# Waits that a cache used to drop, and the unfold steps at one per tile

## The reference

```
xn   = layernorm(x)                      # without weights
q1,q2,k1,k2 = xn @ W1_q.T, ...           # 16 heads of 4 numbers each
L_q  = normalize(q1 ^ q2); L_k = ...     # exterior product: 6 numbers a head
P    = softmax(causal(L_q . J6 L_k / sqrt(6)))
attn = (P @ (xn @ W_v.T + b_v)) @ W_out.T + b_out
W_real, W_imag = unfold(G1_R, G2_R), unfold(G1_I, G2_I)   # two 512 x 512 matrices from small cores
ffn  = complex product of xn's halves with W_real, W_imag, + biases
y    = x + attn + ffn
```

## Time and profile before

| what | value |
|---|---|
| three runs, us | 4673.68, 4672.62, 4688.39; median 4673.68 |
| profiled execution, us | 4680.85 |
| span of its slowest core, us | 4679.7 |
| spans of its cores, us | 4645.7 to 4679.7 |
| PE, PEld busy | 60%, 21% |
| DVE, ACT, POOL busy | 30%, 31%, 3% |
| mean granted PE clock | 0.66 |

### The profile page before, as it was taken

How to read it: one execution, slowest core, us unless ns; L and a number is a source line. 1 busy time by engine, 2 the same in 40 slices (tenths; PEclk the granted TensorE clock), 3 DMA queues, 4 the chain that set the end, 5 groups by cost and what they waited for, 6 DMA issues and landing times.

```text
span 4679.7 us, 33896 instructions; the slowest of 8 cores (4645.7 to 4679.7 us)
## 1 busy us (share of the span) xinstructions
PE 2820.8 (60%) x10528; PEld 970.6 (21%) x10528; DVE 1386.5 (30%) x2833; ACT 1474.0 (31%) x1729; POOL 141.3 (3%) x210
## 2 busy tenths in 40 slices
PE   2358555566656755556655855556665686666665
PEld 1114111121112411111211511112211241111112
DVE  5534333322223234332222323432222231111111
ACT  0000144434331034443332014444333204455550
POOL 2200000000000000000000000000000000000001
PEclk9868655567656955567765875556665695555558
DMA  5602201012100311111100040011110031000004
GB/s 112 47 0 67 91 27 34 28 59 68 45 9 7 57 38 32 34 40 67 63 21 11 15 71 28 28 34 59 63 50 7 5 51 32 14 12 14 12 12 74
DMA packets 87133, 180.13 MB, mean 38 GB/s; under 512 B 41760, under 2 KB 42920, under 8 KB 86960
## 3 DMA queue, kind: packets, MB, share of 16 engines
q0 software_dynamic: 56672, 75.38, 8.7%
q1 hardware_dynamic: 30288, 102.58, 7.3%
HBM read 114.36 MB, written 69.73 MB: 39 GB/s over the span
## 4 chain that ended last, share of the span: by engine, by line
PE 44%; DMA 21%; DVE 14%; ACT 12%; issue 7%; DVEq 0%; SPq 0%; ACTq 0%; POOL 0%; POOLq 0%
PE O L609 18%; DMA cdiv<-rscr 10%; DMA y<-ost 7%; PE S L569 7%; PE F L410 5%; ACT exps L592 5%; PE F L446 4%; DMA rscr<-cdiv 3%; DVE oT L651 3%; ACT cdiv L635 3%; ACT cdiv L633 3%; PE F L453 2%; PE F L336 2%; DVE exps L600 1%; PE F L316 1%
## 5 line engine op out<-in xcount | busy, mean ns | idle before, releaser
L592 ACT ACTIVATE exps<-S 128x1024 bf16<-128x1024 f32 (+3 forms) x1280 | 1119.4, 893 | 2046.7 <-PE O L609 1310.1
L609 PE MATMUL O<-exps,vaug 128*65 128x512 bf16 (+3 forms) x2560 | 1030.9, 503 | 807.6 <-DVE oT L651 479.5
L569 PE MATMUL S<-fqp,fkp 6*128 6x512 bf16 (+3 forms) x2560 | 613.2, 488 | 437.8 <-ACT exps L592 431.8
L609 PEld LDWEIGHTS O<-exps,vaug 128*65 128x65 bf16 x2560 | 229.7, 135 | 1244.6 <-issue 1226.0
L651 DVE TENSOR_TENSOR oT<-O,cdiv 64x512 bf16<-64x512 f32 x256 | 175.0, 684 | 895.4 <-DMA cdiv<-rscr 891.3
L569 PEld LDWEIGHTS S<-fqp,fkp 6*128 6x128 bf16 x2560 | 131.9, 97 | 1154.3 <-issue 1151.8
L600 DVE TENSOR_TENSOR exps<-exps,tri 128x256 bf16<-128x256 bf16 x512 | 143.7, 292 | 725.8 <-ACT exps L592 722.8
L515 PE MATMUL S<-wout,oT 128*128 128x512 bf16 x1024 | 252.8, 407 | 100.0 <-DVE ost L524 90.8
L410 PE MATMUL F<-wv,xnT 128*128 128x256 bf16 x2048 | 233.2, 279 | 0.4 <-DVE vaug L422 0.4
L316 PE MATMUL F<-idt,xnst 128*128 128x128 f32 x512 | 119.9, 413 | 146.2 <-DVE xnst L303 146.2
L410 PEld LDWEIGHTS F<-wv,xnT 128*128 128x128 bf16 x2048 | 190.6, 100 | 48.0 <-issue 7.1
(11 more groups left out here) (75 smaller groups left out, 1961.4 us busy)
## 6 DMA issues: line engine op xcount, KB each, us to landing
y<-ost POOLq DMA_DIRECT2D x128, 512.0 KB, 5.3
x2st<-x SPq DMA_DIRECT2D x64, 512.0 KB, 4.3
cdiv<-rscr SPq DMA_DIRECT2D x128, 256.0 KB, 3.6
xst<-x SPq DMA_DIRECT2D x56, 512.0 KB, 4.4
exps<-x SPq DMA_DIRECT2D x8, 512.0 KB, 4.9
wv<-wvT POOLq DMA_DIRECT2D x8, 256.0 KB, 22.9
wout<-woutT POOLq DMA_DIRECT2D x8, 256.0 KB, 23.7
tascr<-qk POOLq DMA_DIRECT2D x16, 128.0 KB, 2.1
```

What stands on the lines that cost most here:

```text
L569: tS.inc(TE.matmul(S_ps[:, ss * 1024 + j * 512 + soff: ss * 1024 + j * 512 + 512], fk_pad[32 * m4:32 * m4 + 6, kt * 128:kt * 128 + 128], f ...
L592: sS.inc(SE.activation(e_out, e_in, AF.Exp))
L609: ins = TE.matmul(O4[:, j * 512 + off:(j + 1) * 512], vaug[:, kt * 1040 + h * 65: kt * 1040 + h * 65 + 65], exp_sb[:, ss * 1024 + j * 512 ...
```

## The change

Two things are changed.

1. `Sem.wait` no longer remembers anything: every call issues its wait. The waits that come back are all fulfilled when the engine reaches them. Counted over the whole program (each core has the same one), there are 2118 more wait instructions:

| engine | waits before | after | where the new ones stand (with the lines of before) |
|---|---|---|---|
| PE | 2582 | 3780 | V_group 260, scores of a pair 256, A2_tile 227, C_scatter 130, FFN_pass1 106, B2_chunk 76, burst_outproj 70, ahead of L609 for O4 32, B1_chunk 25, unf_step 16 |
| DVE | 2375 | 3069 | FFN_pass1 317, A1_tile 182 (127 of them right ahead of L303), emit_divide 128 (ahead of L651), burst_outproj 67 |
| SP | 625 | 772 | emit_divide 143 (127 of them ahead of L640), A1_tile 4 |
| ACT | 1781 | 1860 | emit_divide 48 (ahead of L633) and one more, exp 30 |
| POOL | 276 | 276 | none |

2. The loop over the 16 tiles of batch 0 issues one unfold step behind each tile where it issued two, and `unf_fin` comes after the loop. Before, the 16 steps stood behind tiles 0 to 7 in pairs (F6, then F7), and `unf_fin` behind tile 8. Now tile 0 has a step in F6, tile 1 one in F7, and so on to tile 15.

No arithmetic is added or taken away, and apart from the unfold steps no instruction changes its place.

```
     def wait(self, eng, n=None):
-        v = self.n if n is None else n
-        k = id(eng)
-        if self.lastw.get(k, -1) >= v:
-            return
-        self.lastw[k] = v
-        eng.wait_ge(self.h, v)
+        eng.wait_ge(self.h, self.n if n is None else n)
```

```
         for tt in range(NT):
             A1_tile(0, tt, tt % 2)
             A2_tile(0, tt)
-            for _ in range(2):
-                if unf_steps:
-                    unf_steps.popleft()()
+            if unf_steps:
+                unf_steps.popleft()()
+        while unf_steps:
+            unf_steps.popleft()()
         for ch in range(4):
             B1_chunk(0, ch)
```

More of the change, by code:

```diff
@@ L80, in __init__ @@
         self.n = 0
-        self.lastw = {}
     def inc(self, instr, k=1):
```

## The result

| | before | after |
|---|---|---|
| median of the runs, us | 4678.82 (8 runs) | 4747.44 (8 runs) |
| ratio, 95% interval | | 1.0142 [1.0125, 1.0159] |
| profiled execution, us | 4680.85 | 4746.13 |
| mean of the 8 cores' spans, us | 4662.3 | 4714.3 |

The changed kernel is 1.4% slower; 1.2% was forecast, 4728 us, with 4697 to 4768 as the range. In the profiled executions the slowest core is 65 us later, the mean core 52 us. In some executions, whatever the kernel, the cores of a die are granted a lower clock and take some per cent longer; the ratios leave these out, while the medians of the experiments hold them, so the two can differ by a few us.

A forecast was written before the change was run, and what follows sets the result against it. Handovers, not a busy engine, bound the kernel, with nearly all 128 divisions in the chain. Waits 47 us plus unfold steps 6.9 gave 54 us on the median of 4673.68: 4728 us, range 4697 to 4768.

The forecast's parts named there:

- nearly free: Rival, whole kernel: queues run ahead, so fulfilled waits cost almost nothing and only unfold steps count; 4679 us, chance 0.13.
- divisions: Division of each head pair, 128 in the chain: new waits on SP, DVE and ACT add 20 us.
- PE's waits exposed in attention: Rival, attention: if PE's queue does not run ahead, each of 668 waits costs 0.10 us; 4806 us, chance 0.10.
- opening, waits and unfold steps: Batch 0's 16 tiles: waits add 3.8 us, unpaired unfold steps net 6.9 us.
- q/k stage of batch 0: Serial q/k steps with PE empty before each: new PE waits behind the blocking one add 2.0 us.
- value stages: All four batches: a fulfilled sem_s wait per group of 8 matmuls, 49 groups a batch at full clock, adds 10 us.
- q/k of later batches and PE's other waits in attention: Attention stages: 6 us for later batches' q/k steps, 5 us for PE's scores, C_scatter, A2_tile, O4 and burst waits.
- DVE outside division and opening: DVE's remaining new waits, such as FFN_pass1's: taken as hidden, 0 us.
- FFN and output stages: FFN and output stages of the batches: no change in length, 0 us.
- The zero for FFN_pass1: FFN_pass1: DVE's and PE's new waits fall into time already spent waiting; 0 us, at worst 4.5.
- The gathers: Started at about 210 us instead of 123.22, they hide behind the q/k stage, which moves no data.

The follow-up runs named there:

- the two SP variants: Kernel before with four more fulfilled SP waits at each write of the reciprocal, behind or ahead of the blocking wait: ratio 1.0062 behind, 0.9999 ahead.
- division cached: Changed kernel with the cache back inside emit_divide alone, 320 waits fewer: 4719.9 us, ratio 1.0085.
- values only: Kernel before with the cache off for PE's two waits in V_group alone, 260 extra waits: 4695.84 us, ratio 1.0019.
- PE's waits only: Kernel before with the cache off for PE alone, 1198 of the 2118 waits: 4708.54 us, ratio 1.005.
- DVE's, no division: Kernel before with the cache off for DVE except in the division, 566 extra waits: 4700.76 us, ratio 1.002.
- the waits only: Kernel before with the cache taken out, all 2118 waits, unfold steps left in pairs: 4753.85 us, ratio 1.0161.

## Why the prediction was right

**The price.** The prices had been read from two tiles that differed by one wait and, for SP, from a division: 0.07 us on DVE, 0.10 on PE, 0.06 on SP. They hold, but for SP's, which is 0.05. In tile 1 of the changed kernel two more on DVE made 0.13, one more on PE 0.15 and in tile 2 0.10, and four on SP made 0.20. The trace also keeps the wait instructions themselves, which no view prints. Ahead of L297 in tile 1 they start at 42.08, 42.15, 42.21 and 42.28, 0.07 apart. Ahead of the write at 581.03 SP's start at 580.88, 580.92 and 580.97, 0.05 apart. In core 0's value stage PE's two start at 1521.49 and 1521.60, 0.11 apart.

**The rule of exposure.** The prediction had a new wait cost something only behind the one that blocks. This is shown by three pairs: the changed kernel and its twin with the blocking wait last (4747 and 4665 us with the same number of waits), the two SP variants, and the value stage (347 and 366 matmuls in 40 us). Of the rivals, "nearly free" fails since the divisions add about 0.14 us each and the whole is 66 us. "PE's waits exposed in attention" fails in full (67 us).

**The terms**, in us, in the means over the cores:

| term | worked out | shown by | measured |
|---|---|---|---|
| divisions | 20 | division cached | 20 to 21 |
| opening, waits and unfold steps | 10.7 | stage A | 10.0 |
| q/k stage of batch 0 | 2.0 | stage q/k | 3.9 |
| value stages | 10 | values stages, values only | 15 |
| q/k of later batches and PE's other waits in attention | 6 + 5 | PE's waits only | 14; 9 to 10 by all executions |
| DVE outside division and opening | 0 | DVE's, no division | 10, within the scatter; about 6 by all executions |
| FFN and output stages | 0 | their stages | -14.5 |

The sum of 54 against 52 for the mean core is nearer than its terms, and that is luck: errors of opposite sign met. Values, q/k stage and DVE's waits were put too low by 5, 2 and some 6 us, and that the FFN and output stages get shorter by 14.5 was not foreseen. The measured terms come from different executions and need not add up to 52; with the two taken over all executions they come to about 50. The value term failed in its count of groups at the full clock, taken from one core and one batch; with 64 groups it would have been 13. The q/k term is larger by 2 us than 20 waits of 0.10 explain; why is not settled, though nearly all of it goes away when the blocking wait is last (+0.2), and the stage scatters by up to 1.4. The zero for FFN_pass1, and for L297 in the paced pieces, rested on DVE having slack there, and perhaps it has not.

The metric is the slowest core, and there the change costs 66 us, 12 more than forecast: the prediction added up one chain and had nothing for a spread between the cores. In the profiled execution the slowest core spent 508.6 us from the issue of the returns to the multiply. Before, it was 478.3 on that core, while the other seven grew by 8 to 16 (128 waits on DVE make 9). With the waits only it is the same: 73 us on the slowest core and 58 in the mean, over all executions. That the slowest core is slower by more than the mean is seen; why its transfers take longer was not tried.

**The gathers.** They had been taken to hide in the q/k stage, and do: with the unfold steps alone the q/k stage grew by 0.4 us, and the first FFN by 0.3.

## What to carry to other kernels

An already fulfilled wait cost 0.05 to 0.11 us here if it stood behind the wait that blocks, in a chain that sets the time, and nothing that could be measured ahead of it. So count not all waits but those between a blocking wait and its instruction, and put the blocking one last. That takes no more instructions. Here the change of order, with no unfold step behind tile 1, made the cached kernel 0.4% faster, and with it the cache no longer made a difference that could be told. To price a small cost of each handover, find two places in the trace where it differs by one, and multiply by the handovers in the chain that ended last. Take the count from all cores.

## What the runs showed of the hardware that was not expected

With PE's 1198 waits in the program, transfers land sooner. A write of y in the output stages took 5.32 us in the median over all cores, against 5.51 before, and loads of x2 4.17 in the mean against 4.27. The output stages are 1.3 to 3.5 us shorter per batch, and batch 0's FFN 3 to 6. It shows in every variant with all of PE's waits, also in the one with the blocking waits last, and in none that leaves PE's queue as it was. The 70 waits of the output stage alone (5.51) and DVE's (5.53) don't do it; the 260 of the values may do a part of it (5.46). In most output stages one or two writes stand out by some 0.7 us or more, at tiles that are the same on all cores and differ between programs. What does it was not found.
